# Reordering GpSimd's gathers at the end of a two-layer graph attention kernel (6144 nodes, one core)

## The reference

```
h = relu(layernorm(x))
scores = where(adj > 0, (h @ W0) @ inp.T, NEG_PAD)
x = x + softmax(scores / 0.07, axis=1) @ inp
h = relu(layernorm(x)) @ W1
e = leaky_relu((h @ a_src)[:, None] + (h @ a_dst)[None, :], 0.2)
valid = (adj > 0) & (h.sum(axis=1) != 0)[None, :]
att = where(valid, softmax(where(valid, e, NEG), axis=1), 0); L = valid.sum(axis=1)
attention = where(att >= 1e-4, att, 0) * L[:, None]      # 0 where a row's top is below 1e-4
x = x + elu(h + attention @ h)
```

## Time and profile before

| | us |
|---|---|
| median of 3 runs | 753.84 (750.98 to 756.42) |
| the profiled execution: its time | 758.33 |
| the profiled execution: its span | 756.7 |
| busy in it: DVE, PE, ACT, POOL | 521.8, 413.3, 410.8, 366.3 |
| granted TensorE clock, mean | 0.751 |

### The profile page before, as it was taken

The page is one execution under the profiler, slowest core; times in us unless marked ns, Lnnn a source line. Parts: engine busy times, 40 slices in busy tenths (PEclk is TensorE's granted clock), DMA queues, the critical chain, the costliest instruction groups (busy, mean ns, idle before and its releaser), DMA issues.

```text
span 756.7 us, 9557 instructions
## 1 busy us (share of the span) xinstructions
PE 413.3 (55%) x2947; PEld 276.4 (37%) x2947; DVE 521.8 (69%) x1921; ACT 410.8 (54%) x424; POOL 366.3 (48%) x424
## 2 busy tenths in 40 slices
PE   3433646566667676767675846647360520416654
PEld 1010213244444343435352524426260520415654
DVE  0019596889898988979893958949822532639994
ACT  4458677777878788888856758662300110012122
POOL 5000140607070606151573765748887887878700
PEclk9577787788988899879795879976565555566786
DMA  8999799999999999999999999932121232223422
GB/s 326 430 412 419 262 305 352 341 352 319 351 353 334 363 336 348 357 349 332 371 321 290 319 306 321 336 110 57 38 59 46 57 76 52 44 58 88 124 83 74
DMA packets 37478, 186.78 MB, mean 247 GB/s; under 512 B 7856, under 2 KB 8112, under 8 KB 18864
## 3 DMA queue, kind: packets, MB, share of 16 engines
q1 hardware_dynamic: 28208, 167.02, 58.8%
q0 software_dynamic: 9216, 19.11, 12.0%
HBM read 179.73 MB, written 6.37 MB: 246 GB/s over the span
## 4 chain that ended last, share of the span: by engine, by line
DVE 30%; POOL 21%; DMA 18%; issue 12%; ACT 9%; PE 8%; SPq 0%; POOLq 0%; DVEq 0%; ACTq 0%
DMA arena<-in_adj 18%; POOL arena L819 12%; ACT arena L873 7%; PE K L1424 4%; POOL mean_w L814 3%; DVE keys L1029 2%; POOL E L819 2%; POOL X L790 2%; DVE s_e L1136 1%; POOL arena L790 1%; DVE mi_w L1175 1%; DVE RTp L1194 1%; PE G L1635 1%; ACT R_all L902 1%; DVE G L1135 1%
## 5 line engine op out<-in xcount | busy, mean ns | idle before, releaser
L873 ACT ACTIVATE arena<-arena,half_c 128x2048 bf16<-128x2048 int32 x144 | 284.5, 1999 | 88.0 <-DMA arena<-in_adj 77.2
L790 POOL DMA_INDIRECT X<-in_L_gnn_input,idx_all x132 | 131.8, 998 | 299.7 <-DVE idx_near L1108 233.9
L1424 PE MATMUL K<-arena,bits 128*128 128x512 bf16 x576 | 174.0, 443 | 22.6 <-ACT arena L873 22.4
L819 POOL DMA_INDIRECT arena<-table,idx_near x96 | 99.5, 1036 | 28.5 <-issue 22.2
L1424 PEld LDWEIGHTS K<-arena,bits 128*128 128x128 bf16 x576 | 60.2, 110 | 97.3 <-ACT arena L873 31.0
L1029 DVE MAX8 keys<-K 128x8 int32<-128x128 f32 x192 | 42.4, 281 | 56.7 <-PE K L1424 56.7
L1422 PE MATMUL K<-key_add,key_one 128*128 128x512 bf16 x48 | 22.4, 466 | 57.8 <-DVE keys L1029 32.1
L819 POOL DMA_INDIRECT E<-table,idx_near x48 | 47.0, 979 | 14.4 <-issue 12.2
L1436 PE MATMUL G<-g,R_all 128*128 128x128 bf16 x324 | 25.3, 228 | 39.3 <-DVE s_e L1136 26.0
L1099 DVE COPY led<-SA 128x396 f32<-128x396 f32 x12 | 6.8, 570 | 56.0 <-PE SA L1482 56.0
L814 POOL MEMSET mean_w<- 128x512 f32 x72 | 38.5, 535 | 2.1
(11 more groups left out here) (245 smaller groups left out, 1031.6 us busy)
## 6 DMA issues: line engine op xcount, KB each, us to landing
arena<-in_adj SPq DMA_DIRECT2D x144, 1024.0 KB, 9.3
table<-hs SPq DMA_DIRECT2D x12, 262.0 KB, 9.1
hs<-table SPq DMA_DIRECT2D x12, 262.0 KB, 2.8
E<-in_L_gnn_input SPq DMA_DIRECT2D x1, 3072.0 KB, 23.9
out_x<-x_all SPq DMA_DIRECT2D x12, 256.0 KB, 2.1
x_all<-in_x SPq DMA_DIRECT2D x1, 2560.0 KB, 17.4
X<-in_L_gnn_input,idx_all POOLq DMA_INDIRECT x132, 6.0
arena<-table,idx_near POOLq DMA_INDIRECT x96, 2.7
```

The lines of the kernel that those rows point to most:

```text
L790: pool.indirect_dma_start(out=x_of(b)[:, e, :], out_offset=None, in_=inp, in_offset=bass.IndirectOffsetOnAxis(ap=idx_all[:, at:at + 1], ax ...
L819: pool.indirect_dma_start(out=E[g][:, t, :], out_offset=None, in_=tables[g], in_offset=bass.IndirectOffsetOnAxis(ap=idx_near[:, t, g:g + 1 ...
L873: nc.scalar.activation(sign[:, load % RING, :], ring[:, load % RING, :], ACT.Sign, bias=half_c[:], scale=1.0).then_inc(signed, 1)
L1424: last = mm(bank_[:], bits[:, third * TB + j, :], sign[:, load % RING, j * FOLD:(j + 1) * FOLD], start=False, stop=(third == G - 1 and j = ...
```

## The change

Third 0's records are issued at steps n = 8 to 11 as 3, 3, 4 and 1 groups (before: 3, 3, 3 and 2). The fourth group of n = 10 waits for `folded` 140, the one of n = 11 for 144. The separate wait for 144 goes. One group of third 1 instead of four stands ahead of `neighbours(11)`. Of third 1, tiles 4 to 24 (before: 16 to 40) come between `neighbours(11)` and `third_stored(2)`. Behind it the thirds 1 and 2 now take turns by eight tiles.

The order after, from the end of the stream: one group of third 0 behind `folded` 140; `neighbours(10)` around the mean of block 9; one group of third 0 behind `folded` 144; the mean of block 10; one group of third 1; `neighbours(11)` around the mean of block 11; five groups of third 1; one of third 0; `third_stored(2)`; four of third 2; two of third 1; four of third 2; then for tiles 32 to 40 and for tiles 40 to 48 two of third 1 and two of third 2. That is 27 groups again.

```
                 EARLY = 8
+                EARLY_GROUPS = [3, 3, 4, 1]
...
                     if n >= EARLY:
-                        for k in range(3):
-                            first = 12 * (n - EARLY) + 4 * k
-                            if first + 4 <= FROM[n]:
-                                pool.wait_ge(folded, min((FROM[n] + SIZES[n]) * G + 2 * k + 2, T * G))
-                                records(0, first, first + 4)
-                pool.wait_ge(folded, T * G)
+                        for k in range(EARLY_GROUPS[n - EARLY]):
+                            first = FEW * (sum(EARLY_GROUPS[:n - EARLY]) + k)
+                            pool.wait_ge(folded, min((FROM[n] + SIZES[n]) * G + 2 * k + 2, T * G))
+                            records(0, first, first + FEW)
                 scale_mean(NB - 2)
                 add_mean(NB - 2)
                 third_stored(1)
-                records(1, 0, 2 * Q)
+                records(1, 0, FEW)
                 neighbours(NB - 1, 0, BG // 2)
                 scale_mean(NB - 1)
                 add_mean(NB - 1)
                 neighbours(NB - 1, BG // 2, BG)
-                records(1, 2 * Q, 5 * Q)
+                records(1, FEW, 3 * Q)
                 records(0, FROM[NB - 1], T)
                 third_stored(2)
                 records(2, 0, 2 * Q)
-                records(1, 5 * Q, T)
-                records(2, 2 * Q, T)
+                records(1, 3 * Q, 4 * Q)
+                records(2, 2 * Q, 4 * Q)
+                for i in range(4, NQ):
+                    records(1, i * Q, (i + 1) * Q)
+                    records(2, i * Q, (i + 1) * Q)
```

## The result

The changed kernel takes 756.3 us in the median of 20 runs (750.7 to 761.87), the kernel before 752.74 in 20 runs beside them. The ratio is 1.006, with a 95% interval of 1.0035 to 1.0086: about 4.5 us longer (the two medians alone differ by 3.6). The forecast was 4.1 longer (757.9 on a median of 753.84), and 0.74 for "within 1%".

What follows compares the result with a forecast made beforehand. Behind the stream of `adj`, GpSimd's gathers and pauses were taken as the bound. Last gather 1.0 + 4.6 + 0.2 = 5.8 us later, less 2.3 slack, plus 0.6 for held gathers: 4.1 longer, 757.9 us; range 752.5 to 763.2.

Steps and rivals of the forecast that it cites:

- Part 1: At n = 10: the moved group waits for the 140th fold and runs behind the gap; list 1.0 us late (0.3 to 1.5).
- Part 2: Fewer groups ahead of `neighbours(11)`: `score(11)` starts 17.4 us earlier and the last store moves with it; no gain at the end.
- Part 3: At `third_stored(2)`: GpSimd arrives before the last store lands, a new stall of 4.6 us (2.5 to 6.5).
- Part 4: In the tail: gathers held beside line 1368 cost 8.5 us against 8.3, so +0.2 (-4.5 to +2.6).
- A: Rival, chance 0.04: the group at n = 10 runs in the gap before 505; store 4.8 us earlier, stall stays: 753.1.
- B: Rival, chance 0.12: no stall, as block 11's chain from `score(11)` to the store runs 4.6 us faster: 753.3.
- C: Rival, chance 0.18: `score(10)` is late, so `neighbours(11)` itself waits for block 11's indices; 3.7 us slower: 761.6.
- D: Rival, chance 0.10: none of tail steps 2 to 4 held, line 1368 starting under 0.05 us ahead; 4.7 us less: 753.2.

Runs made afterwards that it cites:

- the stall filled and doubled: Changed kernel with one group of third 1 moved ahead of `third_stored(2)` (filled) or behind it (doubled): ratios to the kernel before 0.9984 and 1.0159.
- The last set of traces: Four kernels traced apart, the kernel before at 765.36 us: before again 764.45, changed again 777.75, 140th fold first 774.72, no idle time with memset 0.9925.

## Why the prediction was right
**Part 1, the group at n = 10.** Right in kind: released by the 140th fold, behind the gap. I put 1.0 us on it; the trace shows 1.5 (2.27 from the indices against 0.78), my upper bound; the traces of the stall filled and doubled show 0.5. `score(10)` came 3.3 late (28.4 against 25.1; 2.9 forecast), and the indices of block 11 covered it.

**Part 2, `neighbours(11)`.** `score(11)` came 14.9 earlier, not 17.4. 0.5 of the rest is part 1. The larger piece is a gather of 2.29 us held by the line 1194 of block 10, for which I had 0.6 in all, and two of the first group of third 1 took 1.42 and 1.12.

**Part 3, the stall.** 5.7 us against 4.6, inside 2.5 to 6.5. Both sides of the wait came later than forecast: GpSimd arrived at 97.6 from the indices (96.2), and the store landed at 102.6 (100.0), as late as `score(11)`. Filling and doubling the stall show that it is what costs. The last set of traces shows that 6.5 was too low an upper bound (12.4): I had no term for a way from `score(11)` to the store that is longer than the 40 us of before.

**Part 4, the tail.** From the first gather of third 2 to the end of the last one it took 115.8 us; forecast 116.9. Held were 7.2 with one of the three steps held in full, not two. Step 3 cost neither of the two prices that I gave but 1.07: its first multiplication started 0.32 us behind a gather, which passed, and the next gather lost 0.69; beside the second one gather lost 0.38. The last gather came 7.2 later than before (5.8), `take(5)` 5.0 later (4.1 with the 0.6), and what lies behind and what lies behind it was 35.7, not 36.5 (inside the 1.5 that I allowed), with PE's clock higher there. Windows of the tail, which answer to the earlier trace rows:

```profile
734.00:738.00 4.00, 3.82 (x23) 3.83 (x24) 3.97 (x6) 1.45 (x2) 0.00 (x0) 0.69 0.20 70
738.00:743.00 5.00, 3.43 (x27) 3.23 (x25) 3.11 (x6) 2.22 (x4) 0.00 (x0) 0.91 0.35 108
```

The sum from the indices to the end is 256.6 against 252.5: 4.1 longer, as forecast, and 4.5 by the ratio. That the sum fits so closely is luck: the first gather of third 2 came 2.5 later than forecast (0.6 of it allowed for), the tail behind it was 1.1 shorter, and the time behind `take(5)` 0.8 shorter. What held is the mechanism: the two new waits, where they stand and what ends them.

**The rivals.** A was made true by moving the fold. It gives 4.4 us by the times; I had 4.8, and its other half was right, too: the stall stays. B, no stall, did not happen. C's mechanism did not in the first trace of the changed kernel, where block 11's indices came at 38.6 and `neighbours(11)` started at 42.3. In the second they came at 41.4, and GpSimd waited 1.72 us for them instead of its usual 0.3:

```profile
555.21 0.95 POOL L790 DMA_INDIRECT arena<-in_L_gnn_input,idx_all  x1 [1.72 <-DVE idx_near L1110]
```

So the cover of 1.9 us that I worked out is not safe. D's condition, a start under 0.05 us ahead of the gather, held in step 4 alone.

## What to carry to other kernels
When one engine's list is the bound, moving its work forward pays only up to the next wait in the list, and the released work must come back before the list reaches the wait that needs it. So for each step that is moved, list the waits behind it and compute both sides of each: when the engine arrives, and when the releaser does. A gap is only worth what the new wait in front of it leaves; look up which instruction ends that wait, by its count, and where it stands in its own engine's list. Two halves of a change can each hide in the same slack, so measure them together as well as alone. And where an edit moves work ahead of the point from which traces are counted, only the whole time shows its price.

## What the runs showed that I had not expected
A few hundredths of a microsecond decide about 1.5 us. The fourteen traces have 18 gathers of GpSimd, from 470 us on, that start 0.00 to 0.05 us behind a tensor_tensor of 128x1536 on DVE (1.75 to 1.82 us); 17 of them pass in 0.95, and one, at 0.04, takes 2.54. The 145 that start 0.07 us or more behind it, while it runs, all end 0.80 to 0.85 us behind its end. The Trainium skill (SBUF — State Buffer, Who interferes with whom) infers that a tensor_tensor doesn't hold descriptor generation, because the one takes only the read side of the shared pair and the other needs the write side. That isn't borne out here: beside gathers that took 2.51 and 2.42 us a memset put the tensor_tensor a little later, and the longest gather of the tail fell to 2.0. The same section of the Trainium skill also says that a DVE operation with two inputs in SBUF contends with GpSimd's reads. A gather is given its indices in SBUF; whether it is this read that is held, no run here shows.

The chain from `score(11)` to the last store took between 38.7 and 47.1 us in traces of the same instructions.
